# A fused recurrent block: Z products moved into the token banks, X products issued ahead of their chunk, and jobs moved to other units

## What is computed

```python
xz = einsum('bld,ed->bel', layernorm(x), W_in)        # W_in is 1024 x 256
x, z = split(xz, 2)                                   # 512 channels each
xc = silu(causal_conv(x, conv_w, 4 taps) + conv_b)
dt, Bm, Cm = split(xc @ W_x.T, [128, 144])            # Bm, Cm: 16 states
delta = softplus(dt @ W_dt.T + b_dt)
for t:                                                # per channel, for each of 16 states n
    state = exp(delta_t * A_n) * state + delta_t * xc_t * Bm_t[n]
    y_t  += state * Cm_t[n]
y = (y + D * xc) * silu(z)
s = y @ W_out.T + b_out
out = x1 + s * silu(binarized_linear(layernorm(x1)))
```

## Time and profile before

| | us |
|---|---|
| median of 3 runs (1457.07 to 1459.31) | 1457.57 |
| the profiled execution | 1458.92 |
| its span | 1457.1 |
| from the span's start to the first scan of layer 1 | 630.9 |
| chunk 0 (first scan to the first scan of the next) | 104.7 |
| chunks 1 to 5, each on average | 102.4 |
| chunk 6 | 100.7 |
| chunk 7 (first scan to the end of the last) | 91.15 |

### The profile page before, as it was taken

How to read it: one execution, slowest core, us unless ns; L and a number is a source line. 1 busy time by engine, 2 the same in 40 slices (tenths; PEclk the granted TensorE clock), 3 DMA queues, 4 the chain that set the end, 5 groups by cost and what they waited for, 6 DMA issues and landing times.

```text
span 1457.1 us, 23489 instructions
## 1 busy us (share of the span) xinstructions
PE 1378.5 (95%) x8622; PEld 1078.5 (74%) x8652; DVE 1024.6 (70%) x1374; ACT 877.1 (60%) x1433; POOL 904.6 (62%) x578
## 2 busy tenths in 40 slices
PE   7999999999999999988799999999999999999887
PEld 4445469999999999456667767777767768778777
DVE  7755542322322323489799999999999998999996
ACT  4211221111111111399799989999999898999893
POOL 4232211222222222159979989989999989999995
PEclk9999999999999999999999999999999999999999
DMA  9921146766767663122342352534533443523532
GB/s 305 405 82 40 58 142 228 271 241 239 267 246 256 261 239 150 41 65 73 82 102 74 96 120 62 130 88 94 125 82 94 103 102 88 130 75 88 130 91 69
DMA packets 57761, 205.17 MB, mean 141 GB/s; under 512 B 6575, under 2 KB 32815, under 8 KB 48822
## 3 DMA queue, kind: packets, MB, share of 16 engines
q1 hardware_dynamic: 42358, 146.55, 28.7%
q0 software_dynamic: 15296, 57.19, 17.3%
HBM read 141.78 MB, written 31.00 MB: 119 GB/s over the span
## 4 chain that ended last, share of the span: by engine, by line
PE 47%; POOL 24%; DVE 10%; ACT 8%; issue 7%; DMA 3%; SPq 0%; POOLq 0%; DVEq 0%; ACTq 0%
POOL hst L692 18%; PE bank L1505 17%; PE bank L1518 8%; PE bank L1450 7%; DVE hst L1350 4%; POOL dbuT L674 4%; PE bank L1710 3%; ACT dA L895 3%; PE bank L1690 3%; DMA hst<-hst 2%; PE bank L1572 2%; ACT dbuT L884 2%; POOL xpad L652 2%; PE bank L1480 1%; PE bank L1579 1%
## 5 line engine op out<-in xcount | busy, mean ns | idle before, releaser
L1350 DVE TENSOR_TENSOR_SCAN hst<-dA,carry,bank 128x512 f32<-128x512 f32 x512 | 631.7, 1267 | 57.3 <-PE bank L1690 38.8
L692 POOL TENSOR_TENSOR hst<-hst,c_bc 128x2048 f32<-128x2048 f32 x127 | 581.9, 4604 | 21.1 <-DVE hst L1350 6.3
L1690 PEld LDWEIGHTS bank<-ident,dbuT 128*128 128x128 f32 x2048 | 241.9, 142 | 181.3 <-issue 94.8
L895 ACT ACTIVATE dA<-delta,negA 128x512 f32<-128x512 f32 x512 | 357.0, 713 | 6.7 <-DVE hst L1350 6.6
L1690 PE MATMUL bank<-ident,dbuT 128*128 128x128 f32 x2048 | 316.7, 278 | 41.4 <-DVE hst L1350 36.7
L884 ACT ACTIVATE dbuT<-duT,bT 128x512 f32<-128x512 f32 x382 | 271.4, 711 | 8.8 <-PE bank L1690 8.8
L1505 PEld LDWEIGHTS bank<-f_sb,w_gu 128*128 128x128 f32 x2240 | 255.5, 192 | 2.7 <-ACT f_sb L756 1.0
L1505 PE MATMUL bank<-f_sb,w_gu 128*128 128x128 f32 x2240 | 256.0, 275 | 0.7 <-ACT f_sb L756 0.7
L1710 PE MATMUL bank<-ident,hst 128*128 128x128 f32 x1520 | 217.8, 275 | 6.0 <-DMA hst<-hst 5.9
L627 POOL TENSOR_TENSOR x_sb<-x_sb,neg_half 128x1 f32<-128x1 f32 x35 | 23.0, 656 | 260.6 <-DVE x_sb L1179 260.6
L1710 PEld LDWEIGHTS bank<-ident,hst 128*128 128x128 f32 x1520 | 177.5, 143 | 7.3 <-DMA hst<-hst 6.9
(11 more groups left out here) (207 smaller groups left out, 1730.5 us busy)
## 6 DMA issues: line engine op xcount, KB each, us to landing
w_gu<-in_w_gu SPq DMA_DIRECT2D x35, 2048.0 KB, 7.3
c_bc<-c_rows SPq DMA_DIRECT2D x64, 512.0 KB, 4.1
hst<-hst POOLq DMA_DIRECT2D x31, 1024.0 KB, 9.2
sorted_x<-sg_a SPq DMA_DIRECT2D x12, 387.0 KB, 10.7
x_sb<-sorted_x SPq DMA_DIRECT2D x35, 129.0 KB, 7.2
x_sb<-in_x SPq DMA_DIRECT2D x8, 512.0 KB, 7.8
w_d<-in_w_d SPq DMA_DIRECT2D x1, 4096.0 KB, 20.4
x_mix<-x_sb SPq DMA_DIRECT2D x1, 4096.0 KB, 31.0
```

The source lines that it names most:

```text
L692: pool.tensor_tensor(h[:], h[:], c, ALU.mult).then_inc(hc_ready, 1)
L895: act.activation(dA[:, at % DA_BUFS, :], delta[q % B][:, d, :], ACT.Exp, scale=negA[:, d, n:n + 1]).then_inc(dA_ready, 1)
L1350: v.tensor_tensor_scan(h[:, d, :], dA[:, at % DA_BUFS, :], bank[4 + u % 2][:], carry1[q % B][:, n, d:d + 1], ALU.mult, ALU.add).then_inc(s ...
L1690: ins = pe.transpose(bank[4 + u % 2][:, i * P:(i + 1) * P], dbuT[(DS * q + n) % DBU_BUFS][:, i, d * P:(d + 1) * P], ident[:])
```

## The change

Z of chunk q is now made within chunk q, at units 9 to 14, straight into the token banks 0 to 3, as soon as the gate of chunk q - 1 has read a bank out. ACT's `silu_z` reads it there, tile by tile, into `zy`, and `add_skip` (units 17 to 19) opens the sums over it. DVE's copy and the jobs Z0 to Z3 in banks A and B are gone. The first X products of a chunk are issued in the chunk before (the units -4 and -1 of `PE_X`, by `x_slot(q + 1, u - UNITS)`; ahead of the loop for the first one). ACT's silu unit is 21; the gates and z stand there, then unit 22's decay has already been made, six pieces of spreading are asked for in a row (two of them are POOL's), and then come the convolution's silus and the second table load. POOL spreads the states 5, 6, 8 and 11, no longer 4, 7, 10 and 11. Sums, transposes and products stand at other units.

```diff
-POOL_SPREADS = (4, 7, 10, 11)
+POOL_SPREADS = (5, 6, 8, 11)
-PE_X = (0, 1, 2, 3, 7, 8, 9, 10)
-PE_G = (13, 14, 16, 18)
-PE_DT = (21, 23, 24, 26)
-PE_DL = (28, 33, 37, 41)
-PE_BC = (29, 30, 31, 32)
-PE_BT = 47
-PE_DUT = (49, 50, 53, 54)
-PE_Z = (50, 52, 53, 56, 57, 58, 60, 61)
-PE_XN = (60, 62)
-PE_YF = (20, 32, 35, 37)
-PE_OUT = (39, 40, 43, 44, 46, 47, 48, 49)
-PE_SKIP = (9, 10, 11, 12)
-ACT_X = (5, 6, 12, 18)
-ACT_SILU = 24
-ACT_SOFT = (33, 38, 43, 44)
-DVE_CONV = (3, 4, 5, 6, 7, 8, 9, 11, 12, 13, 14, 15)
+PE_X = (-4, -1, 0, 3, 5, 8, 9, 10)
+PE_G = (12, 14, 15, 16)
+PE_DT = (22, 23, 24, 26)
+PE_DL = (28, 34, 36, 41)
+PE_BC = (30, 31, 32, 34)
+PE_BT = 48
+PE_DUT = (51, 53, 54, 55)
+PE_Z = (9, 10, 10, 11, 11, 12, 13, 14)
+PE_XN = (55, 57)
+PE_YF = (21, 32, 35, 37)
+PE_OUT = (39, 40, 42, 44, 46, 47, 49, 51)
+PE_SKIP = (17, 18, 19, 19)
+ACT_X = (3, 6, 11, 16)
+ACT_SILU = 21
+PIECES = 6
+ACT_SOFT = (34, 38, 43, 44)
+DVE_CONV = (2, 3, 4, 5, 6, 8, 9, 10, 11, 12, 13, 14)
 DVE_GATE = (8, 9, 10, 11)
-DVE_DT = 27
-DVE_Z = (53, 58, 59, 62)
-DVE_XN = (61, 63)
-POOL_DU = (7, 9, 10, 11)
+DVE_DT = 28
+DVE_XN = (57, 59)
+POOL_DU = (6, 9, 9, 10)
-SUM_AT = {(13, 0): 4, (13, 1): 4, (13, 2): 5, (13, 3): 5, (14, 0): 5, (14, 1): 6, (14, 2): 6, (14, 3): 6, (15, 0): 7,
-          (15, 1): 7, (15, 2): 8, (15, 3): 8}
+SUM_AT = {(13, 0): 4, (13, 1): 4, (13, 2): 6, (13, 3): 6, (14, 0): 4, (14, 1): 3, (14, 2): 3, (14, 3): 5, (15, 0): 4,
+          (15, 1): 8, (15, 2): 7, (15, 3): 7, (1, 0): 21, (1, 1): 22, (1, 2): 23, (1, 3): 25, (2, 0): 22, (2, 1): 24,
...
-            def silu_z(t):
-                wait_freed(act, t - 1, "Z3")
-                act.activation(zy[t % B][:], zy[t % B][:], ACT.Silu).then_inc(z_ready, 1)
+            def silu_z(t, i):
+                act.wait_ge(z_made, TPC * t + i + 1)
+                act.activation(zy[t % B][:, i, :], bank[i][:], ACT.Silu).then_inc(z_ready, 1)
...
                 if u == ACT_SILU:
+                    for i in range(TPC):
+                        silu_z(q, i)
                     for h in range(2):
                         silu_gate(q, h)
+                if u == ACT_SILU + 1:
                     if q + 1 < CHUNKS:
                         for d in range(DB):
                             silu_conv(q, d)
-                    silu_z(q)
                     act.preload_act_table_set("natural_log_exp_and_others")
...
+            for u in range(-EARLY, 0):
+                x_slot(0, u)
             for q in range(CHUNKS):
                 for u in range(UNITS):
-                    if q > 0 or u > 1:
+                    if (q > 0 or u > 1) and u != ACT_SILU + 1:
                         decay(q, u)
-                    if u + AHEAD < UNITS:
-                        if q > 0 or u + AHEAD >= TPC:
+                    if u == ACT_SILU:
+                        decay(q, u + 1)
+                    if u == ACT_SILU + 1:
+                        for piece in range(u + AHEAD, u + AHEAD + PIECES):
+                            spread_du(q, piece)
+                    elif u + AHEAD < UNITS:
+                        if (q > 0 or u + AHEAD >= TPC) and not ACT_SILU + 1 < u <= ACT_SILU + PIECES:
                             spread_du(q, u + AHEAD)
...
             def gate_y(q, i):
-                v.wait_ge(y_added, ADDED[q, DS - 1, DB - 1])
-                v.wait_ge(z_ready, q + 1)
+                v.wait_ge(y_added, WHOLE[q])
+                v.wait_ge(z_ready, TPC * q + i + 1)
...
-            def z_part(t, i):
-                wait_full(v, t, f"Z{i}")
-                is_freed(v.tensor_copy(zy[(t + 1) % B][:, i, :], place(t, f"Z{i}")[:]), t, f"Z{i}")
...
-            def z_part(t, i, k):
-                M = claim(t, f"Z{i}") if k == 0 else place(t, f"Z{i}")
-                ins = pe.matmul(M[:], xn2T[(t + 1) % B][:, k, i * P:(i + 1) * P], w_in[:, k, DI:2 * DI], start=(k == 0),
-                                stop=(k == KB - 1))
+            def z_part(q, i, k):
+                if k == 0:
+                    wait_past(pe, y_gated, TPC * (q - 1) + i + 1 if q else 0)
+                ins = pe.matmul(bank[i][:], xn2T[q % B][:, k, i * P:(i + 1) * P], w_in[:, k, DI:2 * DI],
+                                start=(k == 0), stop=(k == KB - 1))
                 if k == KB - 1:
-                    is_full(ins, t, f"Z{i}")
+                    ins.then_inc(z_made, 1)
...
             def add_skip(q, i):
 
-                wait_past(pe, y_gated, TPC * (q - 1) + i + 1 if q else 0)
+                pe.wait_ge(z_ready, TPC * q + i + 1)
```

More of the change, by code:

```diff
@@ L129 @@
                 ADDED[q - back, n, d] = len(ADDED) + 1
+WHOLE = [max(at for (chunk, n, d), at in ADDED.items() if chunk == q) for q in range(CHUNKS)]
 CLAIMED = {"DT": PE_DT[0], "BC": PE_BC[0], "BT": PE_BT}
@@ L163 @@
 count = [0] * 8
-for turn in range(FIRST_TURN, CHUNKS + 1):
+for turn in range(FIRST_TURN, 0):
     for name in claims_of(turn):
-        number = FIRST_CLAIMS[name] if turn < 0 else (BANK_A, BANK_B)[BANK_OF[name]]
-        PLACE[turn, name] = number, count[number]
-        count[number] += 1
+        PLACE[turn, name] = FIRST_CLAIMS[name], count[FIRST_CLAIMS[name]]
+        count[FIRST_CLAIMS[name]] += 1
+for turn, name in sorted(((turn, name) for turn in range(CHUNKS + 1) for name in claims_of(turn)),
+                         key=lambda job: UNITS * job[0] + CLAIMED[job[1]]):
+    number = (BANK_A, BANK_B)[BANK_OF[name]]
+    PLACE[turn, name] = number, count[number]
+    count[number] += 1
 def build(nc, a, out):
@@ L860, in slot @@
                         turn_du(q, ACT_DUT.index(u))
+                    if u == ACT_DT:
+                        dt_rows(q)
+                    if u == ACT_BC:
+                        bc(q)
+                if q + 2 < CHUNKS and u in ACT_XN:
+                    turn_xn2(q, ACT_XN.index(u))
                 if u == ACT_SILU:
+                    for i in range(TPC):
+                        silu_z(q, i)
                     for h in range(2):
                         silu_gate(q, h)
+                if u == ACT_SILU + 1:
                     if q + 1 < CHUNKS:
@@ L1281, in result, with conv_slot @@
                          t, f"OUT{h}")
+            def conv_slot(t, u):
+                if t + 1 < CHUNKS and u in DVE_CONV:
+                    conv(t, *divmod(DVE_CONV.index(u), KC - 1))
             def slot(q, u):
+                conv_slot(q, u)
+                conv_slot(q + 1, u - UNITS)
                 if q + 1 < CHUNKS:
-                    if u in DVE_CONV:
-                        conv(q, *divmod(DVE_CONV.index(u), KC - 1))
                     if u == DVE_DT:
@@ L1335, in _ @@
                 first_piece(i)
+            for u in range(-EARLY, 0):
+                conv_slot(0, u)
             for q in range(CHUNKS):
@@ L1648, in out_proj, with x_slot @@
                     is_full(ins, t, f"OUT{h}")
+            def x_slot(t, u):
+                if t + 1 < CHUNKS and u in PE_X:
+                    x_half(t, *divmod(PE_X.index(u), KB))
             def slot(q, u):
-                if q + 1 < CHUNKS and u in PE_X:
-                    x_half(q, *divmod(PE_X.index(u), KB))
+                x_slot(q, u)
+                x_slot(q + 1, u - UNITS)
                 if u in PE_G:
@@ L1726, in _ @@
                     x_half(-1, d, k)
-            for i in range(2):
-                for k in range(KB):
-                    z_part(-1, i, k)
             for d in range(2):
@@ L1741, in _ @@
             turn_du(-1, 0)
-            z_part(-1, 2, 1)
             turn_b(-1)
             turn_du(-1, 1)
-            for k in range(KB):
-                z_part(-1, 3, k)
             for d in range(2, DB):
                 turn_du(-1, d)
-            for i in range(2):
-                wait_freed(pe, -1, f"Z{2 + i}")
             for d in range(DB):
@@ L1759, in _ @@
                         spread(q + 1, 0)
-                    if u in PE_SKIP:
-                        add_skip(q, PE_SKIP.index(u))
+                    for part in range(TPC * KB):
+                        if PE_Z[part] == u:
+                            z_part(q, *divmod(part, KB))
+                    for i in range(TPC):
+                        if PE_SKIP[i] == u:
+                            add_skip(q, i)
                     for back, n, d in (SUMS_AT if q + 1 < CHUNKS else SUMS_LAST)[u]:
```

57 lines of the change are left out of this document (33 added, 24 removed), and 4 rows, old and new, of the table SUM_AT.

## The result

The changed kernel takes 1449.84 us (median of 4 runs, 1448.12 to 1450.50), the kernel before in the same session 1457.95 us (median of 4, 1457.07 to 1459.31). The ratio is 0.9937, 95% interval 0.9925 to 0.9949: 8.1 us less, more than the 0.2% that this measurement can tell. The profiled execution took 1449.39 us with a span of 1447.6, 9.5 less than the span before.

What follows compares the result with a forecast made beforehand. A loop through scan 15, POOL's states 3 to 9 and scan 52 was taken to set the 102.1 us period. Savings 11.0 + 1.4 + 2.5 - 1.6 = 13.3 gave 1444 us, range 1434 to 1459.

Steps and rivals of the forecast that it cites:

- the loop over POOL's states 3 to 9 and scan 52: Scan 15, POOL's states, merge transfer, scan 52, back to scan 15: sets the period at 102.1 us, falls to 97.6.
- The period, 100.2 forecast: Inner chunks: longest path 99.8 us plus 0.4 for three loops close together, a saving of 2.2 a chunk.
- Its work is the same 99.4: POOL in an inner chunk: spreads at other states, own work unchanged at 99.4 us.
- the PE/DVE path: Inner chunk, larger of PE's and DVE's work by groups of units: 100.8 us before, 99.8 after.
- Units 0 to 15: Start of an inner chunk: more PE work and the first Z's wait for a gate lose 1.2 us.
- Units 24 to 63: Rest of an inner chunk: 57.1 us instead of 60.6, with units 52 to 63 falling from 19.1 to 16.1.
- The silu block: ACT behind decay 22: 11.7 us long, scan 23 at 41.0 instead of 37.9, DVE standing 2.4.
- The rival by which it takes the gain back: ACT's silus late or followed by 2 us more gaps: 101.9 us a chunk, 1454 in all; chance 0.18.
- the price of reading z in PSUM: ACT's four silus of z take 2.4 us instead of 1.90 for one, 0.5 more, hidden elsewhere.
- POOL alone, 1438: PE covers ACT's stand and POOL's 99.4 us sets the inner period: 20 us saved; chance 0.20.
- Slower, 1466: Units 9 to 14: PE waits 1.35 us for each of four gates, 103.7 a chunk; chance 0.11.
- Chunks 0, 6 and 7: Outer chunks: chunk 0 with what is ahead saves 2.5 us, chunk 6 saves 1.4, chunk 7 loses 1.6.

Runs made afterwards that it cites:

- du_at_7: The kernel after with one number of POOL_DU back, so POOL makes its first delta times u behind state 7 instead of state 6: 1443.35 us.
- after_short_z_silu: The kernel after with the four silus of Z only 8 columns wide from chunk 2 on: 101.13 us a chunk on average against 101.12.

## Why the prediction was right, and where its sum was off

**Direction, place and mechanism.** Forecast was 1444, measured 1449.84, inside the range, and "faster" as the sum had it. That the loop over POOL's states 3 to 9 and scan 52 stops being the last, through the spread taken out from between them, is shown from both sides. POOL's wait of 2.72 is gone, and is back at 2.70 with the old states. The transfer that scan 52 needs landed 0.12 us ahead of it in each of chunks 1 to 5 before, 1.7 to 2.2 us ahead in the kernel after, and 0.12 again with the old states. What the forecast doesn't have is that scan 4 then waits for the transfer of state 13.

**The period, 100.2 forecast, 101.12 measured.** 2.2 a chunk was forecast and 1.28 came, 4.6 us over chunks 1 to 5, with 0.5 more in chunk 6; that is more than the 3.8 by which the spans miss the 13.3. Most of the rest of the distance from 1444 is the scatter of the profiled executions: they lay 0.97 above the median before and 0.45 below it after, so 9.5 us of span are 8.1 between the medians. The step that failed is "Its work is the same 99.4": POOL's four deltas were counted as work and not as waits. The diff moves the first of them a state earlier, while my own working had scan 23 come 3 us later than before. Both push on one place, and the instruction was not asked what it waits for. The prediction's own sign, POOL waiting under 1 us a chunk, was not met (1.3 in chunk 3, 0.99 of it for delta). `du_at_7` gives 0.54 a chunk of the 0.92 back. The other 0.38 lie in the PE/DVE path, forecast at 99.8 and measured at 100.46 in that kernel's undisturbed chunks.

**Within that path two terms were mis-sized, against each other.** Units 0 to 15 were to cost 1.2 and took 29.49 in chunk 3, the best of the five, 29.8 on average (29.03 in chunk 3 with the delta moved, against 29.15 before): the wait of the first Z product for the gate doesn't show, PE went back to back from unit 4 to the skip. Units 24 to 63 were to take 57.1, and took 58.6 with scan 24 as the start; 0.9 of it lies in units 52 to 63, 17.0 instead of 16.1, where DVE's 12 scans and 3 small operations alone are 16.0 and the sum of larger halves left no room for a handover. The sum was short there before as well: 60.6 for units 24 to 63, where chunk 3 took 63.0, 1.3 of it the wait for the transfer. The 0.3 by which it was short over the whole chunk hid this, since what it had too little there it had too much elsewhere.

**The silu block.** Its length (11.7 forecast, 12.28 measured), scan 23 (41.0 against 40.87) and DVE's stand (2.4 against 1.80) came near the forecast, scan 23 partly by luck: the block is 0.6 longer, and started 27.8 us into the chunk instead of 28.5. The rival by which it takes the gain back is excluded by `after_short_z_silu` as far as ACT's own work goes: PE covers it. Of the price of reading z in PSUM, the four silus took 2.06 us busy, the next instruction 1.92 behind the first of them. The Trainium skill (VectorE: DVE Perf Modes, section on the trn2 errata), from which 2.3 was estimated, is above that by a fifth, and by the trace the reading from PSUM cost ACT nothing over the 1.90 of one silu from SBUF.

**POOL alone, 1438.** It did not come: with the wait for delta gone and PE's Z work nearly gone too, the chunks at the higher clock are still 100.13, not 99.4, and POOL still waits 0.5 for scans in them. The copies show how little busy time alone says here. In the kernel before DVE is the busiest of DVE, ACT and POOL in chunk 3 (96.02), and 2.3 us less of it gave 0.3; in the kernel after POOL is (95.14 against 93.61), and 2.85 us more of DVE cost 2.2. The rule of the Trainium skill (Perfetto Trace Analysis, section Identifying the Most-Contended Engine) names DVE in the first, where relieving it gave little, and POOL in the second, where DVE's work counts nearly in full; whether less work on POOL would have given more there was not run.

**Slower, 1466.** Its condition, 24.0 us from POOL's state 15 to scan 15, was not near: from 943.30 to 963.10 are 19.8.

**Chunks 0, 6 and 7.** Chunk 0 with what lies ahead of it was forecast at -2.5 and gave -2.9, though 1.0 of clock went against it; chunk 6 -1.4 and -0.9; chunk 7 +1.6 and +0.7.

## What to carry to other kernels

When a diff moves many jobs, ask of each moved instruction what it waits for, and whether your own sum makes that later: two shifts that are free alone met here in one wait, and one number in a table was worth, by the medians, as much as two thirds of the whole change. A cost that is taken away counts only where no other engine stands in the same units: four copies were worth 0.3 us a chunk before the products moved and 2.2 after. Where chunks that should be alike differ, read more than one: the wait of scan 4 that carried most of the loss does not show in the chunk that I had followed. And parts of such a change need not be gains by themselves; the spreads' states lose 13 us without the rest, and the kernel with all of it loses 25 without them.
